# Biases of batch 1's 64-head attention: added by VectorE after the projection, or put into PSUM by one-row matmuls ahead of it

## The chip, the core and the metric

The kernel runs on one core of a Trainium2 chip. The metric is the device time of one execution in microseconds (us). TensorE (PE) does the matmuls and writes to PSUM, VectorE (DVE) and ScalarE (ACT) read PSUM and SBUF, GpSimd (POOL) works on SBUF, SyncE (SP) issues the DMAs. Each engine takes its instructions strictly in the order in which the program gives them to it, and waits on semaphores where the code says `wait_ge`.

## The reference, cut to what matters

Two layers of a perceiver, on x of 2 batches x 256 rows x 256 columns, with a context of 2 x 4096 x 256. Layer 0 is cross attention over the context, then the 64-head linear attention of this case, then a coupled feed-forward; layer 1 is cross attention, a 16-head attention and a mixture of experts. The attention that is changed:

```
def _L0_attn_ref(x, Wq, bq, Wk, bk, Wv, bv, Wo, bo, beta):    # x is layernorm(x)
    q = heads(x @ Wq.T + bq)          # 64 heads of 4
    k = heads(x @ Wk.T + bk)
    v = heads(x @ Wv.T + bv)
    be = jnp.exp(beta)
    q = jax.nn.softmax(be * q, axis=-1)
    k = jax.nn.softmax(be * k, axis=-1)
    kv = jnp.cumsum(jnp.einsum('zsD,zsd->zsDd', k, v), axis=1)
    kn = jnp.cumsum(k, axis=1)
    num = jnp.einsum('zsD,zsDd->zsd', q, kv)
    den = jnp.sum(q * kn, axis=-1, keepdims=True)
    out = num / den
    return out @ Wo.T + bo
```

## The kernel before

The five engines have one program each. The long stages are the two cross attentions, `attend(0)` and `attend(1)`, whose order is a list written out by hand (`ORDER`); smaller jobs are written as generators and are advanced a step at a time at places given by tables. Between `attend(0)` and `attend(1)` stands `between`: it advances two jobs in turn by a string for each engine (`BETWEEN`), "a" for a step of `attention1` (the 64-head attention of batch 1, `linear_attention(1)`), "y" for a step of `side0` (what is left of batch 0: the end of its feed-forward, then its query projection for layer 1). On TensorE, `between` also puts in matmuls on a tile of ones (`keep_busy`, the tile `ones` of type f16), whose results are not used.

`linear_attention(b)` works on two tiles (t = 0, 1) of 128 rows. In order:

- VectorE: layernorm (statistics, then, after GpSimd's `rstd`, the normalized `xn`, line 1401).
- TensorE: `turn_norm` transposes `xn` into a PSUM bank (line 480); VectorE copies it to `xnT` (line 1408).
- TensorE: values of both tiles (line 525, 4 matmuls of 256 columns) into bank b1; queries and keys (line 528, 2 matmuls of 512 columns for each tile) into bank b0 for t = 0 and b2 for t = 1. Semaphore `a_qkv` rises once for each tile. An f32 matmul appears as two passes (rows) in the trace, a transpose as one.
- VectorE, for each tile: values plus bias into `v2` (line 1449), queries and keys plus bias into `qk2[t]` (line 1450), maximum over each head's 4 elements (line 1454), that subtracted (line 1455, raises `a_sub`).
- ScalarE, for each tile: Exp of `qk2[t]` in place (line 1045, raises `a_exp`).
- VectorE, for each tile: keys' sums, reciprocal and scaling (lines 1461 to 1463, raises `a_soft`). The first of the three waits for `a_exp`.
- GpSimd: the products of keys and values, `F2` (line 1307). TensorE: their cumulative sums (line 542). VectorE: lines 1475 to 1483. TensorE: transposes (line 549) and the output projection (line 555).

For batch 1 the banks b0, b1, b2 are 4, 5 and 6. Banks 1 and 6 are also accumulators of `attend(0)`; they come free when `acc_free` reaches NU.

The feed-forward of batch 0 stands between these steps. Its last cycle has four matmul stages (lines 574, 585, 592, 601) with a ScalarE activation behind each (Gelu at lines 1069, 1076 and 1082, Tanh at line 1092), and then VectorE's lines 1515 to 1518. On ScalarE the Tanh of line 1092 stands directly ahead of the Exp of line 1045, with a table load between the two.

Of the kernel before, what the change touches and what calls it, by code (L numbers as in the profile page):

```python
# [19 lines left out]
ALU = mybir.AluOpType  # L20
ACT = mybir.ActivationFunctionType
AX = mybir.AxisListType
# [4 lines left out]
P = 128  # L27
B, SEQ, D = 2, 256, 256
# [8 lines left out]
NU = NT  # L37
# [126 lines left out]
def acc_bank(u):  # L164

    return 6 if u % 2 == 0 else 1

def side_banks(what, b=0):  # L170
    return (4, 5, 6) if (what, b) == ("a", 1) else (4, 5, 7) if what == "x" or (what, b) == ("l", 1) else (2, 3, 7)
# [34 lines left out]
def build(nc, x, ctx, consts, cols, w_x, w_a, w_ao, b_a, w_f1, w_f2, w_f3, w_f4, w_g1, w_g2, w_g3, w_y, w_yv, b_yv,  # L206
          w_l, w_vo, w_in, w_out, rows6, w_gate, w_e1, b_e1, w_e2, b_e2, consts6, out):
    with ExitStack() as stack:
# [256 lines left out]
        def _(pe):  # L465
# [6 lines left out]
            def turn_norm(what, b):  # L472

                k = NORM[what, b]
                pe.wait_ge(s("xn"), k + 1)
                if k == 0:
                    pe.wait_ge(s("const_in"), 32)
                for c in range(DC):
                    for t in range(2):
                        mm = pe.transpose(ps[:, side_banks(what, b)[0], (c * 2 + t) * P:(c * 2 + t + 1) * P],  # L480
                                          xn_of(what, b)[:, t, c * P:(c + 1) * P], ident)
                mm.then_inc(s("xn_turned"), 1)
# [30 lines left out]

            def linear_attention(b):
                b0, b1, b2 = side_banks("a", b)
                yield
                yield
                turn_norm("a", b)
                yield
                pe.wait_ge(s("xnT"), NORM["a", b] + 1)  # L520
                pe.wait_ge(s("wa_in"), 48)
                lhs = lambda t, c: xnT[:, c, t * P:(t + 1) * P]
                for t in range(2):
                    for c in range(DC):
                        pe.matmul(ps[:, b1, t * D:(t + 1) * D], lhs(t, c), wa[:, c, 512:768], start=(c == 0), stop=(c == DC - 1))
                for t in range(2):
                    for c in range(DC):
                        mm = pe.matmul(ps[:, b0 if t == 0 else b2, :], lhs(t, c), wa[:, c, 0:512],
                                       start=(c == 0), stop=(c == DC - 1))
                    mm.then_inc(s("a_qkv"), 1)  # L530
                    yield
                for _ in range(LA_WAIT):
                    yield
                for t in range(2):

                    pe.wait_ge(s("a_F"), 2 * b + t + 1)
                    for i, (o, f) in enumerate(((ps[:, b0, :], lambda r: F2[:, r, 0:512]), (ps[:, b1, :], lambda r: F2[:, r, 512:1024]),
                                                (ps[:, b2, 0:D], lambda r: qk2[r][:, D:2 * D]))):
                        if t:
                            pe.wait_ge(s("a_o"), 8 * b + i + 1)  # L540
                            pe.matmul(o, ones[:, :], f(0), start=True, stop=False)
                        pe.matmul(o, tri, f(t), start=(t == 0), stop=True).then_inc(s("a_cum"), 1)
                    yield
                    yield
                    yield
                pe.wait_ge(s("a_o"), 8 * b + 8)
                for c in range(DC):
                    for t in range(2):
                        mm = pe.transpose(ps[:, b0, (c * 2 + t) * P:(c * 2 + t + 1) * P], v2[:, t, c * P:(c + 1) * P], ident)
                mm.then_inc(s("a_oT_ps"), 1)  # L550
                yield
                pe.wait_ge(s("a_oT"), b + 1)
                for t in range(2):
                    for c in range(DC):
                        mm = pe.matmul(ps[:, b1, t * D:(t + 1) * D], t2[:, (c * 2 + t) * P:(c * 2 + t + 1) * P], wao[:, c, :],
                                       start=(c == 0), stop=(c == DC - 1))
                mm.then_inc(s("a_out"), 1)
                yield
# [464 lines left out]
        def _(act):  # L1023
# [13 lines left out]
            def linear_attention(b):  # L1037
                yield
                yield
                yield  # L1040
                yield
                for t in range(2):
                    yield
                    act.wait_ge(s("a_sub"), 2 * b + t + 1)
                    act.activation(qk2[t], qk2[t], ACT.Exp, scale=becol).then_inc(s("a_exp"), 1)
                for _ in range(LA_WAIT - 1):
                    yield
                for t in range(2):
                    yield
                    yield  # L1050
                    yield
                act.wait_ge(s("a_oT_ps"), b + 1)
                act.activation(t2, ps[:, side_banks("a", b)[0], :], ACT.Copy).then_inc(s("a_oT"), 1)
                yield
                yield
# [307 lines left out]
        def _(dve):  # L1363
# [73 lines left out]
            def linear_attention(b):  # L1437
                b0, b1, b2 = side_banks("a", b)
                dve.wait_ge(s("wa_in"), 48)
                yield from layernorm("a", b)  # L1440
                yield
                turned("a", b)
                yield
                heads4 = lambda t: qk2[t].rearrange("p (g d) -> p g d", d=D2)
                for t in range(2):

                    n = 2 * b + t
                    dve.wait_ge(s("a_qkv"), n + 1)
                    dve.tensor_tensor(v2[:, t, :], ps[:, b1, t * D:(t + 1) * D], ba[:, 512:768], ALU.add)
                    link(dve.tensor_tensor(qk2[t], ps[:, b0 if t == 0 else b2, :], ba[:, 0:512], ALU.add))  # L1450
                    yield
                    if n:
                        dve.wait_ge(s("a_sub"), n)
                    link(dve.tensor_reduce(s2[:, :], heads4(t), AX.X, ALU.max))
                    publish(dve.tensor_tensor(heads4(t), heads4(t), s2[:, :].unsqueeze(2).broadcast_to([P, P, D2]), ALU.subtract), "a_sub")
                yield
                for t in range(2):

                    dve.wait_ge(s("a_exp"), 2 * b + t + 1)
                    keys, ksum = heads4(t)[:, H2:2 * H2, :], s2[:, 0:H2]  # L1460
                    link(dve.tensor_reduce(ksum, keys, AX.X, ALU.add))
                    link(dve.reciprocal(ksum, ksum))
                    publish(dve.tensor_tensor(keys, keys, ksum.unsqueeze(2).broadcast_to([P, H2, D2]), ALU.mult), "a_soft")
                    yield
                for _ in range(LA_WAIT - 3):
                    yield
                for t in range(2):
                    n = 2 * b + t
                    q4 = qk2[t][:, 0:D].rearrange("p (h a) -> p h a", a=D2)
                    t4 = t2.rearrange("p (h d a) -> p h d a", a=D2, d=D2)  # L1470
                    for half in range(2):
                        hs = slice(half * 32, half * 32 + 32)
                        cum = ps[:, (b0, b1)[half], :].rearrange("p (h d a) -> p h d a", a=D2, d=D2)
                        dve.wait_ge(s("a_cum"), 3 * n + half + 1)
                        publish(dve.tensor_tensor(t4, cum, q4[:, hs, :].unsqueeze(2).broadcast_to([P, 32, D2, D2]), ALU.mult), "a_o")
                        link(dve.tensor_reduce(v2[:, t, half * P:(half + 1) * P], t2.rearrange("p (g a) -> p g a", a=D2), AX.X, ALU.add))
                        yield
                    dve.wait_ge(s("a_cum"), 3 * n + 3)
                    publish(dve.tensor_tensor(t2[:, 0:D], ps[:, b2, 0:D], qk2[t][:, 0:D], ALU.mult), "a_o")
                    link(dve.tensor_reduce(s2[:, 0:H2], t2[:, 0:D].rearrange("p (h a) -> p h a", a=D2), AX.X, ALU.add))  # L1480
                    link(dve.reciprocal(s2[:, 0:H2], s2[:, 0:H2]))
                    v3 = v2[:, t, :].rearrange("p (h d) -> p h d", d=D2)
                    publish(dve.tensor_tensor(v3, v3, s2[:, 0:H2].unsqueeze(2).broadcast_to([P, H2, D2]), ALU.mult), "a_o")
                    yield
                yield
                dve.wait_ge(s("a_out"), b + 1)
                xs = X[:, 2 * b:2 * b + 2, :]
                dve.wait_ge(s("x_bo"), b + 1)
                link(dve.tensor_tensor(xs, xs, bank(b1, a=2), ALU.add))
                yield  # L1490
# [479 lines left out]
```

## Time and profile before

| | |
|---|---|
| median of 3 runs | 568.9 us (568.12 to 569.2) |
| the profiled execution's own time | 568.82 us |
| its span, first to last instruction | 566.9 us |
| TensorE busy | 521.0 us (92%) |
| VectorE busy | 356.4 us (63%) |
| ScalarE busy | 280.4 us (49%) |
| GpSimd busy | 75.6 us (13%) |
| mean granted TensorE clock | 0.981 |

The time lies 1.9 us above the span; what comes before the first and after the last instruction is in it. Busy shares are means over the whole span. The work that is changed lies between 164 and 200 us.

### The profile page before, as it was taken

What the parts mean: (1) busy time and instruction counts of PE and PEld (TensorE: products, weight loads), DVE (VectorE), ACT (ScalarE), POOL (GpSimd) and SP (SyncE); (2) the same over time, 40 slices, a digit from 0 to 9 for tenths busy, and PEclk for the clock granted to TensorE, in tenths of its full rate; (3) what the DMA queues carried; (4) which work ended last, traced back from release to release, by engine and by line L of the source; (5) the groups of instructions that cost most, each with busy time, mean ns of one, the idle gap of its engine ahead of it and who ended that gap; (6) DMA issues with size and microseconds to landing.
All of it is one profiled execution on the core that took longest, in us unless ns stands there. A gap on an engine that the chain in (4) does not pass through costs nothing.

```text
span 566.9 us, 9396 instructions
## 1 busy us (share of the span) xinstructions
PE 521.0 (92%) x3556; PEld 358.0 (63%) x3556; DVE 356.4 (63%) x855; ACT 280.4 (49%) x608; POOL 75.6 (13%) x66
## 2 busy tenths in 40 slices
PE   8799998998998999999989989799999999887992
PEld 6455664565666655657545767688888778664551
DVE  4774646963647864475465565788878787744335
ACT  3676862536632037484367736788855444011110
POOL 0025041200011100000002220323201111200001
PEclk9999999997999999999999999999999999979997
DMA  8974552000000010000410040223183005950001
GB/s 270 304 210 89 113 122 64 1 2 1 1 0 1 1 28 0 1 2 0 163 62 1 1 150 1 75 61 90 52 317 139 1 1 195 348 201 1 1 0 39
DMA packets 45198, 44.07 MB, mean 78 GB/s; under 512 B 18656, under 2 KB 41184, under 8 KB 45024
## 3 DMA queue, kind: packets, MB, share of 16 engines
q1 hardware_dynamic: 45152, 43.45, 25.0%
q8 instruction: 29, 0.48, 0.3%
q14 instruction: 17, 0.14, 0.1%
HBM read 38.73 MB, written 0.52 MB: 69 GB/s over the span
## 4 chain that ended last, share of the span: by engine, by line
PE 65%; DVE 17%; issue 10%; ACT 5%; POOL 1%; DMA 1%; SPq 0%; DVEq 0%; ACTq 0%; POOLq 0%
PE ps L648 10%; PE ps L677 8%; PE ps L785 7%; PE ps L801 7%; PE ps L662 4%; PE ps L679 4%; PE ps L770 3%; PE ps L951 3%; PE ps L736 3%; PE ps L976 2%; PE ps L758 2%; PE ps L871 1%; DVE mx L1541 1%; PE ps L497 1%; PE ps L574 1%
## 5 line engine op out<-in xcount | busy, mean ns | idle before, releaser
L648 PE MATMUL ps<-ctx_tr,qtl 128*128 128x512 f16 x384 | 91.2, 379 | 2.4 <-ACT arena L1126 1.9
L1541 DVE TENSOR_REDUCE mx<-arena 128x1 f32<-128x512 f32 x64 | 43.2, 682 | 32.2 <-ACT arena L1126 31.9
L648 PEld LDWEIGHTS ps<-ctx_tr,qtl 128*128 128x128 f16 x384 | 36.6, 98 | 41.1 <-issue 5.1
L677 PE MATMUL ps<-ctx_nat,pth 128*128 128x512 f16 x172 | 59.5, 385 | 0.0
L1126 ACT ACTIVATE arena<-ps 128x512 f32<-128x512 f32 x64 | 38.0, 595 | 41.2 <-PE ps L648 41.0
L1111 ACT ACTIVATE arena<-arena,small 128x512 f32<-128x512 f32 x64 | 45.7, 714 | 6.6 <-DVE small L1550 6.5
L679 PE MATMUL ps<-ctx_nat,ptl 128*128 128x256 f16 x172 | 47.5, 276 | 0.0
L801 PE MATMUL ps<-arena,ctx_tr 128*128 128x256 f16 x384 | 47.2, 273 | 0.1
L1555 DVE TENSOR_TENSOR ptl<-ps,pth 128x512 f16<-128x512 f32 x43 | 29.5, 688 | 26.6 <-ACT pth L1119 26.5
L662 PE MATMUL ps<-const,arena 128*128 128x128 f32 x256 | 39.4, 277 | 4.3 <-ACT arena L1111 3.0
L1290 POOL TENSOR_TENSOR rstd<-mv,col 128x2 f32<-128x2 f32 x13 | 9.0, 694 | 245.1 <-DVE mv L1395 245.0
L801 PEld LDWEIGHTS ps<-arena,ctx_tr 128*128 128x128 f16 x384 | 37.5, 98 | 4.6 <-DVE ctx_tr L1708 0.3
L662 PEld LDWEIGHTS ps<-const,arena 128*128 128x128 f32 x256 | 30.4, 142 | 15.5 <-ACT arena L1111 7.0
L1197 ACT ACTIVATE pth<-ps 128x512 f16<-128x512 f32 x32 | 19.0, 594 | 33.3 <-PE ps L770 33.3
L470 PE MATMUL ps<-ones 128*128 128x256 f16 x244 | 32.2, 293 | 1.1 <-DVE ones L1886 1.1
L1190 ACT ACTIVATE ctx_tr<-ps,small 128x256 f32<-128x256 f32 x64 | 29.6, 470 | 5.7 <-DVE work L1647 5.6
L1119 ACT ACTIVATE pth<-ps 128x512 f16<-128x512 f32 x43 | 25.4, 590 | 14.1 <-PE ps L662 14.0
L470 PEld LDWEIGHTS ps<-ones 128*128 128x128 f16 x244 | 25.5, 106 | 6.6 <-DVE ones L1886 1.1
L677 PE MATMUL ps<-ctx_nat,arena 128*128 128x512 f16 x84 | 29.1, 385 | 0.0
L1647 DVE TENSOR_SCALAR_CACHE_REDUCE work<-ps 128x256 f16<-128x256 f32 x64 | 24.4, 418 | 6.4 <-PE ps L758 6.3
L677 PEld LDWEIGHTS ps<-ctx_nat,pth 128*128 128x128 f16 x172 | 17.0, 99 | 17.2 <-issue 1.9
L1555 DVE TENSOR_TENSOR arena<-ps,arena 128x512 f16<-128x512 f32 x21 | 14.5, 689 | 20.4 <-ACT arena L1119 20.3
(293 smaller groups left out, 1039.4 us busy)
## 6 DMA issues: line engine op xcount, KB each, us to landing
ctx_nat<-in_w_e SPq DMA_DIRECT2D x8, 1024.0 KB, 7.5
ctx_tr<-in_w_e SPq DMA_DIRECT2D x6, 1024.0 KB, 11.5
work<-in_ctx SPq DMA_DIRECT2D x8, 512.0 KB, 5.4
ctx_tr<-in_ctx SPq DMA_DIRECT2D x8, 512.0 KB, 7.3
work<-in_w_vo SPq DMA_DIRECT2D x8, 512.0 KB, 3.9
ctx_nat<-in_w_l SPq DMA_DIRECT2D x4, 512.0 KB, 5.2
arena<-in_w_e SPq DMA_DIRECT2D x2, 1024.0 KB, 7.4
wts<-in_rows SPq DMA_DIRECT2D x1, 1024.0 KB, 14.5
```

What stands on the lines that cost most here:

```text
L470: pe.matmul(ps[:, to, 0:SEQ], o[:, 0:P], o, start=True, stop=True, skip_group_check=True)
L648: mm = pe.matmul(ps[:, n % 2, :], qtl[:, qh, d, u * P:(u + 1) * P], CT[:, t0:t0 + KT, kh, d, :], start=(i == 0 and d == 0), stop=(i == 2 a ...
L662: mm = pe.transpose(ps[:, 4 + j % 2, i * P:(i + 1) * P], S[:, (j) % SRING, i * P:(i + 1) * P], ident)
L677: pe.matmul(ps[:, acc, :], PH[j % PRING][:, i * P:(i + 1) * P], CN[:, t].rearrange("p h d -> p (h d)"), start=(c == 0 and i == 0), stop=Fa ...
L679: mm = pe.matmul(ps[:, acc, 0:D], PL[j % PRING][:, i * P:(i + 1) * P], CN[:, t, 0, :], start=False, stop=(c == NCH - 1 and i == KT - 1), s ...
L785: mm = pe.matmul(ps[:, 4 + i % 2, d * SEQ:(d + 1) * SEQ], xl5[b][:, xh, u, d * P:(d + 1) * P], pt[:, i % 2, pu], start=(n == 0), stop=(n = ...
L801: mm = pe.matmul(ps[:, 6 + b, t * D:(t + 1) * D], oT5[:, i % 2, oh, c, p * P:(p + 1) * P], vo[:, h, vh, c, :], start=(i % H5 == 0 and p == ...
L1111: act.activation(S[:, j % SRING, :], S[:, j % SRING, :], ACT.Exp, bias=ebias[:, u:u + 1], scale=SCALES[L], accum_out=ls[:, u, c:c + 1]).th ...
L1126: act.activation(S[:, n % SRING, :], ps[:, n % 2, :], ACT.Copy).then_inc(s("score_copied"), 1)
L1190: act.activation(P5[:, i % 2, t, :], ps[:, i % 2, t * SEQ:(t + 1) * SEQ], ACT.Exp, bias=nb5[:, i % 2, t:t + 1], scale=1.0 / 16, accum_out= ...
L1541: dve.tensor_reduce(mx[:, u, c:c + 1], S[:, n % SRING, :], AX.X, ALU.max).then_inc(s("score_max"), 1)
L1555: dve.tensor_tensor(PL[j % PRING], ps[:, 4 + j % 2, :], PH[j % PRING], ALU.subtract).then_inc(s("pt_lo"), 1)
```

## The change

For batch 1 alone, the biases bq, bk and bv (row 0 of `ba`, columns 0 to 768) are written into the PSUM banks by four matmuls of one row (`ones[0:1, :]` by a piece of the bias row), and the projections accumulate on top of them. Queries and keys of t = 0 go to bank 1 in place of bank 4. VectorE takes the maximum, and subtracts it, straight from PSUM. The values are copied from PSUM to `v2` by ScalarE. TensorE gets a wait for `acc_free` (banks 1 and 6 must be free) ahead of the four matmuls, and a wait for both Exps ahead of the cumulative sum that overwrites bank b1.

```diff
+QK_BANK = 1
...
             def linear_attention(b):
                 b0, b1, b2 = side_banks("a", b)
-                yield
-                yield
+                first = QK_BANK if b else b0
+                yield
+                yield
+                if b:
+                    pe.wait_ge(s("acc_free"), NU)
+                    row = lambda a, z: ba[0:1, a:z]
+                    for to, a, z in ((ps[:, b1, 0:D], 512, 768), (ps[:, first, :], 0, 512), (ps[:, b2, :], 0, 512)):
+                        pe.matmul(to, ones[0:1, :], row(a, z), start=True, stop=False, skip_group_check=True)
+                    pe.matmul(ps[:, b1, D:2 * D], ones[0:1, :], row(512, 768), start=False, stop=False, skip_group_check=True)
                 turn_norm("a", b)
                 yield
                 pe.wait_ge(s("xnT"), NORM["a", b] + 1)
...
-                        pe.matmul(ps[:, b1, t * D:(t + 1) * D], lhs(t, c), wa[:, c, 512:768], start=(c == 0), stop=(c == DC - 1))
+                        pe.matmul(ps[:, b1, t * D:(t + 1) * D], lhs(t, c), wa[:, c, 512:768], start=(c == 0 and b == 0), stop=(c == DC - 1),
+                                  skip_group_check=True)
...
-                        mm = pe.matmul(ps[:, b0 if t == 0 else b2, :], lhs(t, c), wa[:, c, 0:512],
-                                       start=(c == 0), stop=(c == DC - 1))
+                        mm = pe.matmul(ps[:, first if t == 0 else b2, :], lhs(t, c), wa[:, c, 0:512],
+                                       start=(c == 0 and b == 0), stop=(c == DC - 1), skip_group_check=True)
...
+                        if b and not t and i == 1:
+                            pe.wait_ge(s("a_exp"), 2 * b + 2)
...
                 for t in range(2):
+                    if b:
+                        act.wait_ge(s("a_qkv"), 2 * b + t + 1)
+                        act.activation(v2[:, t, :], ps[:, side_banks("a", b)[1], t * D:(t + 1) * D], ACT.Copy)
                     yield
                     act.wait_ge(s("a_sub"), 2 * b + t + 1)
                     act.activation(qk2[t], qk2[t], ACT.Exp, scale=becol).then_inc(s("a_exp"), 1)
...
                     dve.wait_ge(s("a_qkv"), n + 1)
-                    dve.tensor_tensor(v2[:, t, :], ps[:, b1, t * D:(t + 1) * D], ba[:, 512:768], ALU.add)
-                    link(dve.tensor_tensor(qk2[t], ps[:, b0 if t == 0 else b2, :], ba[:, 0:512], ALU.add))
+                    raw = heads4(t)
+                    if b:
+                        raw = ps[:, QK_BANK if t == 0 else b2, :].rearrange("p (g d) -> p g d", d=D2)
+                    else:
+                        dve.tensor_tensor(v2[:, t, :], ps[:, b1, t * D:(t + 1) * D], ba[:, 512:768], ALU.add)
+                        link(dve.tensor_tensor(qk2[t], ps[:, b0 if t == 0 else b2, :], ba[:, 0:512], ALU.add))
...
-                    link(dve.tensor_reduce(s2[:, :], heads4(t), AX.X, ALU.max))
-                    publish(dve.tensor_tensor(heads4(t), heads4(t), s2[:, :].unsqueeze(2).broadcast_to([P, P, D2]), ALU.subtract), "a_sub")
+                    link(dve.tensor_reduce(s2[:, :], raw, AX.X, ALU.max))
+                    publish(dve.tensor_tensor(heads4(t), raw, s2[:, :].unsqueeze(2).broadcast_to([P, P, D2]), ALU.subtract), "a_sub")
```

The order of TensorE's instructions in the stage between the two cross attentions, before. L470 are the matmuls on the tile of ones, L574 to L601 belong to the feed-forward of batch 0, L480 are the transposes of `xn` of batch 1, L525 and L528 its projection (one row here is one matmul of the program, an f32 one being two passes in the trace):

```order
L574 MATMUL ps<-arena,wts 128x256 x4
L470 MATMUL ps<-ones 128x256 x6
L585 MATMUL ps<-wts 128x256 x2
L480 MATMUL ps<-const,work 128x128 x4
L592 MATMUL ps<-wts 64x256
L525 MATMUL ps<-arena,work 128x256 x4
L528 MATMUL ps<-arena,work 128x512 x4
L601 MATMUL ps<-wts 128x256
```

The same place on TensorE in the changed kernel, whose line numbers are higher (L598 was L585, L483 was L480, L614 was L601):

```order
L587 MATMUL ps<-arena,wts 128x256 x4
L473 MATMUL ps<-ones 128x256 x6
L598 MATMUL ps<-wts 128x256 x2
L526 MATMUL ps<-wts,ones 128x256
L526 MATMUL ps<-wts,ones 128x512 x2
L527 MATMUL ps<-wts,ones 128x256
L483 MATMUL ps<-const,work 128x128 x4
L605 MATMUL ps<-wts 64x256
L535 MATMUL ps<-arena,work 128x256 x4
L539 MATMUL ps<-arena,work 128x512 x4
L614 MATMUL ps<-wts 128x256
```

The four bias matmuls (L526, L527) stand between the second feed-forward stage and the transposes; nothing else moved on TensorE.

The order of ScalarE's instructions at the same place, before (L1069 to L1092 are the feed-forward's activations, L1045 the Exps, L1053 the copy behind the transposes of line 549):

```order
L1069 ACTIVATE wts<-ps,col 128x256 x2
L1076 ACTIVATE wts<-ps,col 128x256
L1082 ACTIVATE wts<-ps,col 64x256
L1092 ACTIVATE wts<-ps,small 128x256
L1045 ACT_TABLE_LOAD
L1045 ACTIVATE work<-work,small 128x512 x2
L1053 ACTIVATE work<-ps 128x512
```

And in the changed kernel (L1108 was L1092, L1061 was L1045):

```order
L1085 ACTIVATE wts<-ps,col 128x256 x2
L1092 ACTIVATE wts<-ps,col 128x256
L1098 ACTIVATE wts<-ps,col 64x256
L1108 ACTIVATE wts<-ps,small 128x256
L1058 ACTIVATE work<-ps 128x256
L1061 ACT_TABLE_LOAD
L1061 ACTIVATE work<-work,small 128x512
L1058 ACTIVATE work<-ps 128x256
L1061 ACTIVATE work<-work,small 128x512
L1069 ACTIVATE work<-ps 128x512
```

The copy of the first tile's values (L1058) stands between the Tanh and the table load, that of the second tile between the two Exps.

## Rows read from the trace of the kernel before

**Rows 1.** The page: engines' busy time, and the chain that ended last by engine.

```profile
PE 521.0 (92%) x3556; PEld 358.0 (63%) x3556; DVE 356.4 (63%) x855; ACT 280.4 (49%) x608; POOL 75.6 (13%) x66
PE 65%; DVE 17%; issue 10%; ACT 5%; POOL 1%; DMA 1%; SPq 0%; DVEq 0%; ACTq 0%; POOLq 0%
```

**Rows 2.** The chain in order of time, 164 to 180 us: start, duration, what.

```profile
168.14 0.74 DVE work L1401 x2
168.93 0.67 PE ps L480 x4
...
170.37 1.99 PE ps L525 x8
172.37 1.73 PE ps L528 x4
...
179.12 0.43 DVE s L1461
```

**Rows 3.** Timeline of TensorE, 166 to 196 us: start, duration, line, operation.

```profile
167.84 1.03 PE L585 MATMUL ps<-wts 128*128 128x256 f32 x4
...
172.20 3.60 PE L528 MATMUL ps<-arena,work 128*128 128x512 f32 x8
175.73 0.70 PE L601 MATMUL ps<-wts 64*128 64x256 f32 x2
176.36 6.50 PE L470 MATMUL ps<-ones 128*128 128x256 f16 x58
```

**Rows 4.** Timeline of ScalarE, 166 to 196 us.

```profile
176.46 0.47 ACT L1092 ACTIVATE wts<-ps,small 128x256 f32<-128x256 f32 x1 [5.79 <-PE ps L601]
176.96 1.28 ACT L1045 ACT_TABLE_LOAD   x1
178.25 0.72 ACT L1045 ACTIVATE work<-work,small 128x512 f32<-128x512 f32 x1
179.12 0.72 ACT L1045 ACTIVATE work<-work,small 128x512 f32<-128x512 f32 x1
```

**Rows 5.** Timeline of VectorE, 166 to 196 us.

```profile
174.12 0.42 DVE L1449 TENSOR_TENSOR work<-ps,wts 128x256 f32<-128x256 f32 x1 [3.80 <-PE ps L528]
174.46 0.68 DVE L1450 TENSOR_TENSOR work<-ps,wts 128x512 f32<-128x512 f32 x1
175.18 0.69 DVE L1454 TENSOR_REDUCE s<-work 128x128 f32<-128x512 f32 x1
175.90 0.69 DVE L1455 TENSOR_TENSOR work<-work,s 128x512 f32<-128x512 f32 x1
176.62 0.42 DVE L1449 TENSOR_TENSOR work<-ps,wts 128x256 f32<-128x256 f32 x1
```

**Rows 6.** The chain, 150 to 205 and 199 to 230 us.

```profile
184.50 0.43 DVE s L1461
...
200.69 0.67 PE ps L549 x4
...
204.03 7.77 PE ps L648 x36
```

**Rows 7.** Groups by line and shape, 160 to 205 us: busy us, mean ns of one.

```profile
L528 PE MATMUL ps<-arena,work 128*128 128x512 f32 x8 | 3.6, 592 | 0.0
...
L601 PE MATMUL ps<-wts 64*128 64x256 f32 x4 | 1.4, 428 | 0.0
...
L585 PE MATMUL ps<-wts 128*128 128x256 f32 x4 | 1.0, 380 | 0.0
```

**Rows 8.** Timeline of ScalarE, 214 to 226 us: two activations back to back, and one alone.

```profile
216.66 0.84 ACT L1069 ACTIVATE work<-ps,col 128x256 f32<-128x256 f32 x2
...
218.35 0.47 ACT L1076 ACTIVATE work<-ps,col 128x256 f32<-128x256 f32 x1 [0.22 <-PE ps L585]
```

**Rows 9.** Stretches: PE, PEld, DVE, ACT, POOL busy, granted clock, DMA share, GB/s.

```profile
180.00:184.00 4.00, 2.86 (x27) 2.31 (x24) 3.86 (x6) 0.00 (x0) 2.01 (x1) 1.00 0.00 0
...
500.00:505.00 5.00, 5.00 (x21) 3.62 (x20) 2.15 (x7) 0.00 (x0) 0.21 (x1) 0.54 0.90 347
```

## The prediction, made before the changed kernel ran

> **What bounds the kernel now.** I read the page first. TensorE is busy 92% of the span, and the chain of work that ended last is TensorE for 65% and VectorE for 17% of it [rows 1]. That is a mean over stages, so it doesn't say what the edited stage waits for. I went on to the chain in order of time around the edit. At 168 us it goes from the layernorm (L1401) to TensorE's transposes (L480), which start at 168.93, then through the projection (L525, L528). From there on it is VectorE's, until L1461 at 179.12 and beyond [rows 2]. VectorE's own timeline shows why: it waits 3.80 us for L528, starts L1449 at 174.12 and from there its instructions stand end to end [rows 5]. The chain leaves VectorE for TensorE's L549 only at 200.69, and the scores of the next cross attention (L648) start at 204.03 [rows 6], behind all of this in TensorE's program. So a microsecond that L1461 starts later is a microsecond later for the rest of the kernel.
>
> The third view is ScalarE's timeline. Its Exp of the first tile ends at 178.25 + 0.72 = 178.97, only 0.15 before VectorE starts L1461, which needs it. And this Exp does not start when its data is there: it stands behind the Tanh (176.46), which waited 5.79 us for TensorE's L601, and behind a table load of 1.28 [rows 4]. L601 in turn is behind the projection, at 175.73 [rows 3]. So two paths end at L1461 nearly together: projection, VectorE's eight instructions, L1461; and projection, L601, Tanh, table load, Exp, L1461. A gain on the first one alone is worth at most 0.15 us.
>
> **The change part by part.**
>
> *Taken from VectorE.* L1449 and L1450 of both tiles. From L1449's start to L1454's start are 175.18 - 174.12 = 1.06 us [rows 5], twice 2.12 us. This is on the first path only.
>
> *VectorE reads PSUM for the maximum and the subtraction.* No reduction from PSUM is in these rows. The nearest: L1450 reads 512 f32 columns from PSUM in 0.68, L1455 the same amount from SBUF in 0.69, L1454 reduces from SBUF in 0.69 [rows 5]. I take no difference; the upper bound, a doubled reduction, would add 0.7 for each tile and, as is shown below, would still be covered.
>
> *Four bias matmuls on TensorE.* They are eight passes: four of 256 columns and four of 512. Four passes of 256 columns (L585) took 1.03 with one alone at 0.380, so the step from one to the next is (1.03 - 0.38) / 3 = 0.217. Eight passes of 512 took 3.60 with one at 0.592: (3.60 - 0.59) / 7 = 0.430 [rows 3, 7]. Sum: 4 x 0.217 + 4 x 0.430 = 2.59 us. Those are passes over 128 rows, and these have one. The nearest row with fewer is L601: 64 rows, 256 columns, 428 ns mean for one, against 380 with 128 rows [rows 7]. Half the rows made it no shorter, so I take the full price. The bounds are zero, if a pass costs by rows, and, if the eight do not overlap at all, 4 x 0.380 + 4 x 0.592 = 3.89 us.
>
> The Trainium skill bears on this step ("TensorE: Matmul & The Clock Gate", § Why this matters for your kernels): its row on small contractions says that one matmul of 32 rows takes as long as one of 128. The trace shows the same for 64 rows, and nothing in it reaches down to one row. By the page the bias passes cost the full 2.59 and the kernel is slower; by a price that goes by rows they would be nearly free.
>
> *Where do they lie?* In TensorE's order they are behind L585 and ahead of L480. L585's last pass starts at about 167.84 + 3 x 0.217 = 168.49, so the first bias pass can start at 168.71. `acc_free` is no wait, since VectorE publishes it before it begins this layernorm. The passes end their turn at 168.71 + 2.59 = 171.30, and L480, which was ready at 168.93 [rows 2, 3], starts then: 2.37 us late. Only 0.22 us is hidden, in the gap between the two. TensorE has no idle time here that could take the rest; the layernorm it used to wait for is what the passes now overlap, and it is nearly over. Everything behind L480 moves by 2.37: the copy to `xnT`, L525, L528, and L601 too.
>
> *The copy of the values on ScalarE.* The first one stands behind the Tanh and ahead of the table load, thus on the second path. Two such activations back to back took 0.84, one alone 0.47: one more costs 0.37 [rows 8]. (0 if it were covered, 0.5 if it did not overlap the Tanh.) The second copy stands between the two Exps: the second Exp ended at 179.84 [rows 4], and its reader is VectorE's second L1461 at 184.50 [rows 6]. It has 4.7 us, and needs no more than a few tenths of them. The new wait of TensorE for both Exps is far behind them and costs nothing.
>
> *The sum at L1461.* Second path: the Exp ends at 178.97 + 2.37 + 0.37 = 181.71, and VectorE starts some 0.03 later, at 181.74. First path: the second tile's projection ended at 172.20 + 3.60 = 175.80, now 178.17, and then come one reduction and one subtraction, 2 x 0.72: 179.61. VectorE therefore waits 2.1 us for the Exp: what it saves turns into this wait, and a slower read of PSUM would vanish in it. L1461 starts at 181.74 in place of 179.12: **+2.62 us**. Terms: 2.37 (bias passes) + 0.37 (copy) + 0.03 (hand-over) - 0.15 (VectorE had been the later one). From there VectorE's instructions are the same, and so are TensorE's behind them.
>
> The profiled execution took 568.82 us, 0.08 under the median of 568.9. 568.82 + 2.62 = 571.44, from the median 571.52. I say **571.5 us**, 0.46% slower.
>
> **The rivals.** What a measurement of this kernel can tell from no change I take as 0.2%, 1.14 us.
>
> *Passes of one row are cheap* (10%). For it: they multiply 1/128 of the cells, and no row is under 64 rows. Against it: L601. With a price of zero the Exp still gets the copy: 0.37 + 0.03 - 0.15 = +0.25, 569.1 us, no change. It becomes a measurable loss once the eight passes cost over 1.1 us.
>
> *The delay is taken up later* (3%). A wait for something that did not move, say a DMA, would absorb it. The chain has 1% of DMA in all [rows 1], and the transfers behind 204 us are issued on semaphores of the work itself. Result within 1.1 us of 568.9.
>
> *The bias passes don't overlap one another* (6%). Weights of one row might not be loaded ahead. 3.89 in place of 2.59 gives +3.92: 572.7 us.
>
> *TensorE's clock falls in this stretch* (3%). It was granted in full here, with TensorE busy 2.86 of 4 us at the loosest place; at 500 to 505 us it was 0.54, near 1.2 GHz [rows 9]. If the bias passes, L525 and the first half of L528 ran at half speed, they would take 2.59 + 1.99 + 1.73 = 6.3 us more: about 577.7 us.
>
> *The saving on VectorE comes through: faster* (4%). The mechanism: the Exp isn't the gate, because ScalarE has its table loaded and the Tanh done early. The place is L1461; the price is the first path alone. With bias passes at their full price that path gives 179.61, +0.49; it ends on the fast side only if they cost less than 1.9 us as well. At zero it gives 175.82 + 1.44 = 177.26, 1.86 earlier: 567.0 us. The point from which it decides: the Exp would have to end by 177.3, 1.7 us before its row, but the Tanh alone ended at 176.93 and the load takes 1.28 [rows 4]. That is why it gets little; part of the 4% is for something in a later stage that falls better by luck.
>
> **How the numbers follow.** The forecast holds 74%; its own range is 570.8 to 572.3, from the copy's bounds (0 to 0.5), the spread of the three runs of before, and some tenths for the stages behind. Adding the case without overlap makes 80%; the edges of the cheap-pass case are reached from 570.2. So the range is 570.2 to 573.0. Slower by over 0.2%: 74 + 6 + 3 = 83%. Within 0.2%: 10 + 3 = 13%. Faster: 4%.
>
> **What the profile after would show.** The eight bias passes between L585's and L480's counterparts, 0.22 and 0.43 apart, and the transposes starting near 171.3 (right), or within 0.3 of 169 (the cheap-pass case). VectorE's first reduction starting near 176.5 and its duration near 0.69. The Tanh near 178.8, the copy, the table load near 179.7, the Exp to 181.7. An idle time of VectorE of about 2.1 us that ends with the Exp, ahead of L1461's counterpart: this is the step that says the saving is lost. If VectorE has no such wait, the reading of the two paths is wrong. The scores of the next cross attention start near 206.6. The prediction fails if a one-row pass costs much less than a full one, or if the clock moves.

## The result, and the profile after

The changed kernel took 574.91 us (median of 11 runs, 570.65 to 576.66), the kernel before 568.66 us (median of 11 runs): ratio 1.0101, 95% interval 1.0083 to 1.0119, 1.0% slower. Predicted were 571.5 us, in a range of 570.2 to 573.0. The direction was right and the size was not: the loss is 6.25 us where 2.6 were forecast, 2.4 times as much. Two executions far outside the rest, of two kernels of the experiments, are left out of what follows: one of 909 us at a clock of 0.55 throughout, and one of 2511 us.

The 11 runs fall into two groups. Four of them (570.65, 571.02, 571.44, 572.52 us) have a mean granted TensorE clock of 0.981 to 0.982; seven (574.4 to 576.66 us) have 0.972 to 0.976. The profiled execution (574.40 us) is one of the seven. The middle of the four, 571.23, is 2.6 us above the kernel before, which is what was forecast. Whether those four escaped the cost that is found below is not shown, since none of them was profiled.

The page of the changed kernel: busy time by engine, the granted clock in 40 slices, the chain that ended last by engine.

```profile
PE 526.6 (92%) x3564; PEld 361.1 (63%) x3564; DVE 354.7 (62%) x851; ACT 280.8 (49%) x610; POOL 75.7 (13%) x66
...
PEclk9999999998998999999999989999999999989997
...
PE 74%; DVE 15%; ACT 6%; issue 3%; POOL 1%; DMA 1%; SPq 0%; DVEq 0%; ACTq 0%; POOLq 0%
```

Against [rows 1] TensorE is busy 5.6 us longer and VectorE 1.7 us less. A slice is 14.3 us wide, and the 8 in the thirteenth (172 to 186 us) is at the changed place, where the kernel before had full clock.

TensorE's timeline of the changed kernel, 164 to 206 us: start, duration, line.

```profile
165.78 1.03 PE L598 MATMUL ps<-wts 128*128 128x256 f32 x4
166.74 2.41 PE L526 MATMUL ps<-wts,ones 1*128 1x256 f32 x6
169.00 0.76 PE L527 MATMUL ps<-wts,ones 1*128 1x256 f32 x2
169.69 1.11 PE L483 MATMUL ps<-const,work 128*128 128x128 f32 x4
...
171.78 3.78 PE L535 MATMUL ps<-arena,work 128*128 128x256 f32 x8
175.36 3.98 PE L539 MATMUL ps<-arena,work 128*128 128x512 f32 x8
179.26 0.70 PE L614 MATMUL ps<-wts 64*128 64x256 f32 x2
```

The eight bias passes (L526 and L527, one row, `1*128`) stand between the feed-forward's stage and the transposes, and the first six of them run at the pace that was worked out: L526's start to L527's is 2.26 us. Then everything gets slow. The transposes (L483) take 1.11 in place of 0.67, and the eight passes over the values (L535) 3.78 in place of 1.99 [rows 2]. L539 takes 3.98 in place of 3.60 [rows 3], and what follows it is at the old pace again.

The same stretches by window, with the granted clock third from the end.

```profile
168.00:170.00 2.00, 2.00 (x7) 0.87 (x6) 0.00 (x0) 0.00 (x0) 0.17 (x1) 0.82 0.00 0
170.00:172.00 2.00, 2.00 (x7) 0.91 (x6) 0.69 (x1) 0.11 (x1) 0.00 (x0) 0.50 0.00 0
172.00:174.00 2.00, 2.00 (x5) 1.63 (x6) 0.00 (x0) 0.36 (x1) 0.00 (x0) 0.50 0.04 8
174.00:176.00 2.00, 2.00 (x5) 1.35 (x4) 0.00 (x0) 0.00 (x0) 0.00 (x0) 0.50 0.00 0
176.00:180.00 4.00, 4.00 (x11) 1.55 (x10) 1.96 (x3) 0.00 (x1) 0.00 (x0) 0.99 0.00 0
```

The clock is 0.50, the lower level of 1.2 GHz, from about 169.3 to 176 us. It fell while the bias passes ran, and TensorE was busy the whole time: 2.00 of 2 us in each window, and 4.00 of 4 from 160 to 164 and from 164 to 168 us too. So it isn't idleness that took the clock. At another place a fall does come behind idle time: in the kernel before TensorE is busy 2.44 us of the 4 from 132 to 136 us, and the clock is 0.50 from 136 to 140.

VectorE's and then ScalarE's timeline of the changed kernel. L1424 is the copy behind the transposes (before: L1408), L1474 the reduction from PSUM (L1454), L1481 the keys' sums (L1461); L1108 is the Tanh (L1092), L1058 the new copy, L1061 the Exp (L1045).

```profile
170.84 0.69 DVE L1424 COPY work<-ps 128x512 f32<-128x512 f32 x1 [4.01 <-PE ps L483]
177.65 0.69 DVE L1474 TENSOR_REDUCE s<-ps 128x128 f32<-128x512 f32 x1 [6.12 <-PE ps L539]
...
179.43 0.69 DVE L1474 TENSOR_REDUCE s<-ps 128x128 f32<-128x512 f32 x1 [0.35 <-PE ps L539]
...
182.87 0.42 DVE L1481 TENSOR_REDUCE s<-work 128x64 f32<-128x256 f32 x1 [2.03 <-ACT work L1061]
```

```profile
180.00 0.48 ACT L1108 ACTIVATE wts<-ps,small 128x256 f32<-128x256 f32 x1 [7.64 <-PE ps L614]
180.37 0.38 ACT L1058 ACTIVATE work<-ps 128x256 f32<-128x256 f32 x1
180.75 1.28 ACT L1061 ACT_TABLE_LOAD   x1
182.05 0.72 ACT L1061 ACTIVATE work<-work,small 128x512 f32<-128x512 f32 x1
```

The four adds are gone and the reduction from PSUM takes 0.69, as from SBUF [rows 5]. And VectorE then stands still for 2.03 us until the Exp ends: that is what the removed adds became. Of VectorE's waits, the two for the transposes and for the projection have grown, to 4.01 and 6.12 us (from 0.75 and 3.80), and the 2.03 is new.

GpSimd's timeline is a good ledger of the whole program, since it has few instructions and they are the same ones in both kernels. Before, then after (L1290 and L1306 are the layernorms' `rstd`, L1307 and L1323 the product of keys and values):

```profile
167.42 0.69 POOL L1290 TENSOR_TENSOR rstd<-mv,col 128x2 f32<-128x2 f32 x1 [39.70 <-DVE mv L1395]
...
180.67 2.01 POOL L1307 TENSOR_TENSOR work<-work 128x1024 f32<-128x1024 f32 x1 [10.44 <-DVE work L1463]
...
335.22 0.69 POOL L1290 TENSOR_TENSOR rstd<-mv,col 128x2 f32<-128x2 f32 x1 [5.92 <-DVE mv L1395]
351.94 1.16 POOL L1337 TENSOR_TENSOR arena<-work,arena 128x512 f16<-128x512 f32 x1 [16.03 <-ACT arena L1171]
```

```profile
165.37 0.69 POOL L1306 TENSOR_TENSOR rstd<-mv,col 128x2 f32<-128x2 f32 x1 [38.11 <-DVE mv L1411]
...
184.41 2.01 POOL L1323 TENSOR_TENSOR work<-work 128x1024 f32<-128x1024 f32 x1 [16.24 <-DVE work L1483]
...
338.99 0.69 POOL L1306 TENSOR_TENSOR rstd<-mv,col 128x2 f32<-128x2 f32 x1 [5.93 <-DVE mv L1411]
357.28 1.16 POOL L1353 TENSOR_TENSOR arena<-work,arena 128x512 f16<-128x512 f32 x1 [17.60 <-ACT arena L1187]
```

From the `rstd` of batch 1's attention to its first product, which I call **the stretch** from here on, it was 180.67 - 167.42 = 13.25 us and is 184.41 - 165.37 = 19.04: +5.79. From there to 335.22 or 338.99 both take the same to 0.03. The rest of the ledger lies in code that is the same in both: the stretch began 2.05 us earlier in this execution, and from 339 to 357 us 1.57 are lost, while the clock is 0.57 at 336 to 340 us. Such stretches of low clock are in the kernel before too, at 136 to 144 and 496 to 508 us, and their place and length differ from one profile to the next. What one is worth can be read from the same ledger: between GpSimd's `rstd` at 127 us and the one that opens the stretch, the kernel before took 40.41 us with the low clock at 136 to 144; four kernels of the experiments, whose code there is the same and whose profiles have full clock there, took 37.36 to 37.38. That is 3.0 us for one fall.

Two cautions follow. The kernel before itself ran in 565.12 to 570.85 us on one chip. With 5.79 us added that is 570.9 to 576.6, nearly all that the changed kernel's 11 runs cover, so its two groups can come from the falls elsewhere as well as from the stretch. And the loss at 336 us is in the four profiles with eight f32 bias passes (0.57 to 0.62 in a window of 4 us) and in none of the other seven; with one profile of each kernel no run says whether that is chance.

### The profile page after: what moved, and what is told of

It is laid out like the page before. It is cut to its first block, busy times and chain, and to the rows that moved or that the text cites. A ratio compares the mean times of both kernels' runs of the same rounds, so it can differ in the third digit from the quotient of the medians.

```text
span 572.6 us, 9409 instructions
## 1 busy us (share of the span) xinstructions
PE 526.6 (92%) x3564; PEld 361.1 (63%) x3564; DVE 354.7 (62%) x851; ACT 280.8 (49%) x610; POOL 75.7 (13%) x66
## 4 chain that ended last, share of the span: by engine, by line
PE 74%; DVE 15%; ACT 6%; issue 3%; POOL 1%; DMA 1%; SPq 0%; DVEq 0%; ACTq 0%; POOLq 0%
PE ps L661 10%; PE ps L690 10%; PE ps L798 7%; PE ps L814 7%; PE ps L675 5%; PE ps L692 5%; PE ps L749 3%; PE ps L783 3%; PE ps L964 3%; PE ps L989 2%; PE ps L587 2%; PE ps L771 2%; PE ps L884 1%; DVE mx L1561 1%; PE ps L598 1%
## 5 line engine op out<-in xcount | busy, mean ns | idle before, releaser
L1306 POOL TENSOR_TENSOR rstd<-mv,col 128x2 f32<-128x2 f32 x13 | 9.0, 696 | 243.1 <-DVE mv L1411 243.0
```

## The experiments

Theory 1: passes that feed one row into the array do not keep TensorE's clock up, and this is the part of the loss that the forecast lacked. Theory 2: the rest is as forecast, that is, the passes' turn on TensorE costs 2.4 us, and VectorE's saving is lost because the Exp gates it. In the medians below "before" is the kernel before on the same chip. The stretch is read from the one profile of each kernel, and so is the clock in it.

**Bias passes alone, on the kernel before.** VectorE's adds stay; the one-row matmuls write banks that nobody reads.

```diff
+                if b:
+                    pe.wait_ge(s("acc_free"), NU)
+                    for to, a, z in ((ps[:, 1, 0:D], 512, 768), (ps[:, 1, :], 0, 512), (ps[:, 6, :], 0, 512), (ps[:, 1, 0:D], 512, 768)):
+                        pe.matmul(to, ones[0:1, :], row(a, z), start=True, stop=True, skip_group_check=True)
                 turn_norm("a", b)
```

> The kernel before, with all its VectorE adds, and with the wait and four one-row matmuls of the same sizes ahead of the transposes; they write PSUM banks that are overwritten or unused, so nothing of the result changes. Theory 1: the passes alone bring both costs, 2.4 us of TensorE's turn and, in most runs, the clock: runs at about 571.1 us (568.7 + 2.37) and runs at about 574.7. Rival (the accumulation on top of the bias, or the PSUM reads, matter): 571.1 us or less in all runs, with the clock at 1.00 from 168 to 180 us.

Measured: 574.07 us (6 runs) against 568.61, ratio 1.0082 (1.0050 to 1.0113). Four runs at 573.97 to 575.41 and two at 570.26 and 571.35: two groups again. The stretch took 18.83 us, +5.58. Its clock, by window:

```profile
168.00:172.00 4.00, 4.00 (x12) 1.74 (x10) 0.52 (x1) 0.00 (x0) 0.69 (x1) 0.71 0.00 0
172.00:176.00 4.00, 4.00 (x11) 2.87 (x10) 0.17 (x1) 0.47 (x1) 0.00 (x0) 0.50 0.01 4
```

The passes alone bring both costs, the turn and the clock. Accumulating on top of them and reading PSUM are not needed for either.

**The same passes over 128 rows.** The identity by the bias rows, which stand in all 128 partitions of `ba`, gives the same sum.

```diff
-                    row = lambda a, z: ba[0:1, a:z]
+                    row = lambda a, z: ba[:, a:z]
...
-                        pe.matmul(to, ones[0:1, :], row(a, z), start=True, stop=False, skip_group_check=True)
+                        pe.matmul(to, ident, row(a, z), start=True, stop=False, skip_group_check=True)
```

> The changed kernel, with the same eight bias passes at the same place, but over 128 rows: the identity by the bias rows that stand in all 128 partitions of the bias tile. The result is the same. Theory 1 (TensorE's clock fell because of passes that feed one row): the granted clock stays 1.00 from 168 to 180 us, the first reduction from PSUM starts 2.4 us later after the layernorm than in the kernel before, and every run is 2 to 3.2 us above the kernel before, about 571.3 us, with none near 575. Rival (the clock fell for another cause, such as a stretch without matmuls nearby or the new wait): 575 us in more than half of the runs and a clock near 0.5 behind the bias passes, as in the changed kernel (574.9 us median).

Measured: ratio 1.0047 (1.0023 to 1.0071) against 568.61 us, seven runs between 569.22 and 572.92 us and none near 575. Its profiled execution was the one of 909 us, so the kernel was run again.

> The same kernel as the one with bias passes over 128 rows, for a profile at full clock. Theory 1 (the clock fell because the passes feed one row): clock 1.00 from 168 to 180 us, the transposes 2.4 us later after the layernorm, the Exp ends 2.7 us later, runs around 571.5 us. Rival: a clock near 0.5 right behind the bias passes and runs near 575.

Measured: 571.48 us (6 runs) against 568.19, ratio 1.0071 (1.0044 to 1.0099), the slowest at 573.96. TensorE's timeline and one window of it:

```profile
165.33 2.31 PE L526 MATMUL ps<-wts,const 128*128 128x256 f32 x6
167.48 0.59 PE L527 MATMUL ps<-wts,const 128*128 128x256 f32 x2
167.91 0.60 PE L483 MATMUL ps<-const,work 128*128 128x128 f32 x4
...
169.30 1.99 PE L535 MATMUL ps<-arena,work 128*128 128x256 f32 x8 [0.21 <-DVE work L1424]
```

```profile
168.00:172.00 4.00, 3.79 (x18) 2.48 (x17) 0.69 (x1) 0.47 (x1) 0.00 (x0) 1.00 0.02 4
```

The clock is 1.00 and L535 takes 1.99 again. The stretch took 15.75 us, +2.50, against a forecast of +2.62. The program is the same but for what the bias passes read, the identity and 128 bias rows in place of a row of ones and one bias row: 19.04 - 15.75 = 3.29 us is what the fall of the clock cost in the profiled execution. TensorE is busy no more here (3.79 of 4 us), and this kernel has one non-zero weight in a column, just as the one-row passes have. What differs is the rows that are fed. The times bear it out: the interval of the changed kernel, 1.0083 to 1.0119, does not meet that of the first of these two experiments, 1.0023 to 1.0071, and meets that of the second, 1.0044 to 1.0099, only at its upper end.

**64 rows.** The upper half of the identity by 64 bias rows; rows 64 to 127 of each tile get no bias.

```diff
+                        pe.matmul(to, const[0:64, 0, :], ba[0:64, a:z], start=True, stop=False, skip_group_check=True)
```

> The changed kernel with the eight bias passes over 64 rows: half of the identity by 64 bias rows, so that rows 64 to 127 of each tile of batch 1 get no bias. The passes take as long as with one row or 128. Theory 1: the clock stays up, as with 128 rows, about 571.3 us; should it fall as with one row, some runs near 575 us, so the number of rows between one and 64 isn't what tells, and only full passes keep it. Rival of e1: 575 us here as there.

Measured: 571.97 us (6 runs, 571.02 to 573.6) against 568.61, ratio 1.0063 (1.0043 to 1.0084); clock 1.00 in the stretch, which took 16.10 us, +2.85. The passes and what follows them cost 0.35 more here than with 128 rows. Where between one row and 64 it turns was not tried.

**No bias matmuls at all.** The changed kernel without them and their wait: bq, bk and bv of batch 1 are left out.

```diff
-                if b:
-                    pe.wait_ge(s("acc_free"), NU)
...
-                    pe.matmul(ps[:, b1, D:2 * D], ones[0:1, :], row(512, 768), start=False, stop=False, skip_group_check=True)
```

> The changed kernel without the bias matmuls and their wait: the biases bq, bk, bv of batch 1 are left out. VectorE's four adds are gone, ScalarE's copy stands ahead of the table load. Theory 1 (Tanh, copy, table load, Exp gate VectorE, its saving becomes a wait): 568.7 + 0.25 = 568.9 us, within 0.6; VectorE idles about 1.6 us ahead of its keys' sums, ended by the Exp. Rival (the saving counts): 566.8 us, and no such wait.

Measured: 568.24 us (12 runs) against 568.61, ratio 1.0006 (0.9987 to 1.0024). Four adds fewer on VectorE, and nothing gained. The stretch took 13.47 us, +0.22, and VectorE's timeline has the wait:

```profile
179.40 0.42 DVE L1475 TENSOR_REDUCE s<-work 128x64 f32<-128x256 f32 x1 [2.02 <-ACT work L1055]
```

I had written 1.6 us for this wait; it is 2.02. Its end is what counts, and the stretch moved by 0.22 where 0.25 was expected.

**The feed-forward's last matmul ahead of the projection, on the kernel before.** This takes the Exp out of VectorE's way.

```diff
                         pe.matmul(ps[:, b1, t * D:(t + 1) * D], lhs(t, c), wa[:, c, 512:768], start=(c == 0), stop=(c == DC - 1))
+                if b:
+                    yield
                 for t in range(2):
...
-    "aayyayaaaayyyyayaaayyaaay",
+    "aayyayayaaaayyyayaaayyaaay",
```

> The kernel before, with one move: the feed-forward's last matmul (line 601) stands ahead of the projection of queries and keys, not behind it. Its Tanh and the table load then run while the projection does, so the Exp no longer waits for them. Theory 2 (two paths of nearly equal length, the adds on VectorE being the other): the projection comes 0.43 us later, VectorE is never stopped by the Exp, and the time is 568.6 + 0.43 = 569.0 us. Rival (the Exp was what held VectorE in the kernel before): faster than before by over 1 us.

Measured: 569.66 us (12 runs, 566.2 to 573.88) against 568.19, ratio 1.0029 (1.0005 to 1.0053), where 569.0 us was expected: not faster, so the Exp was not what held the kernel before. But the move costs more than 0.43. The stretch took 14.08, +0.83, and VectorE's wait for the projection grew from 3.80 [rows 5] by 0.82:

```profile
171.87 0.42 DVE L1451 TENSOR_TENSOR work<-ps,wts 128x256 f32<-128x256 f32 x1 [4.62 <-PE ps L530]
```

So this matmul of 64 rows among ones of 128 cost its two passes, 0.43 us, and some 0.4 us at the seams.

**The change with cheap passes.** Biases as f16 high and low halves, made by GpSimd and stacked on partitions 0 to 63 and 64 to 127, against a tile of 1/64: four f16 passes over all 128 rows. They replace the six matmuls on the tile of ones ahead of line 585's stage. First with line 601's matmul where it was.

```diff
+                    pe.wait_ge(s("b16"), 3)
+                    for to, a, z in ((ps[:, b1, 0:D], 512, 768), (ps[:, first, :], 0, 512), (ps[:, b2, :], 0, 512)):
+                        pe.matmul(to, inv64[:, :], ba16[:, a:z], start=True, stop=False, skip_group_check=True)
...
+            pool.memset(inv64[:, :], 1.0 / 64).then_inc(s("b16"), 1)
+            pool.tensor_copy(ba16[:, :], ba[:, 0:3 * D]).then_inc(s("b16"), 1)
+            pool.wait_ge(s("b16"), 2)
+            pool.tensor_tensor(ba16[64:128, :], ba[64:128, 0:3 * D], ba16[64:128, :], ALU.subtract).then_inc(s("b16"), 1)
```

> As the f16 version, but with line 601's matmul where it was, behind the projection. Theory 2: the Exp gates VectorE again, with the values' copy ahead of the table load: 568.6 + 0.25 = 568.9 us, and VectorE waits some 1.6 us for the Exp. Rival (the place of the matmul doesn't matter): the same time as the version with it moved, 567.2 us.

Measured: 569.15 us (12 runs) against 568.19, ratio 1.0035 (1.0011 to 1.0059); 568.9 was expected. The stretch took 13.47, +0.22, just as without biases: the passes are free, VectorE's saving is still lost, and it waits 2.03 us for the Exp.

**The same with line 601's matmul early.**

> The changed kernel, with the biases as f16 high and low halves (made by GpSimd long before, high on partitions 0 to 63, low on 64 to 127, against a tile of 1/64), so four f16 passes over 128 rows in place of eight; they stand in the place of six matmuls on the tile of ones, ahead of line 585's stage; and line 601's matmul ahead of the projection of queries and keys. Theory 2: the passes cost nothing (0.64 us in place of 0.64), the gate is lifted, VectorE's saving counts: 0.43 later for the projection, then 179.12 - 177.7 = 1.4 us earlier at the keys' sums, 567.2 us. Rival (the saving is lost for another reason): 568.6 or more.

Measured: 570.57 us (12 runs) against 568.19, ratio 1.0047 (1.0024 to 1.0070). A miss in the whole, where 567.2 was expected, though the stretch took 12.30, 0.95 less than before: the gate is lifted and the saving counts, less the 0.8 of the moved matmul. A loss lies 40 us earlier, in both f16 kernels: from the `rstd` at 127 us to the stretch this one took 42.55 us, 2.14 more than the kernel before with the same fall of the clock on the way. This is VectorE's normalization for the feed-forward in the one of the experiment ahead, beside GpSimd's new work (it took 0.73 before):

```profile
127.72 2.75 DVE L1425 TENSOR_SCALAR wts<-X,mv,rstd 128x256 f32<-128x256 f32 x2 [0.24 <-POOL rstd L1308]
```

GpSimd's cast and subtraction, 0.82 and 1.64 us, held VectorE for 2.0 us. The kernel before has the same at another place: its L1515 took 0.41 us at 162.58 and 2.20 at 180.62, beside GpSimd's product of 2.01. The Trainium skill has this ("SBUF — State Buffer", § SBUF: two separate sides): some of VectorE's instructions and GpSimd's lock a shared pair of ports, and whichever comes second blocks until the other's instruction is done; the 2.75 and the 2.20 agree.

**GpSimd's work later.** One wait more, `pool.wait_ge(s("f_gs"), 1)`.

> The f16 version with line 601's matmul early, but GpSimd makes the halves later, after the feed-forward's first Gelu of the context, when VectorE does not run its normalization. In the earlier version that normalization took 2.75 us in place of 0.73 beside GpSimd, and this is where its 2 us went. Theory 2: 0.95 us earlier at the keys' sums, as measured there, and nothing lost elsewhere: about 567.5 us in the median of runs of the kernel before at 568.4. Rival (the loss was in the changed order, or in the clock alone): 569.5 or more, and a normalization that takes 0.73 us with the time no better.

Measured: 568.75 us (12 runs) against 568.25, ratio 1.0008 (0.9989 to 1.0028). The normalization takes 0.74 and the stretch 12.30 again. Against the version ahead 1.9 us came back (0.50 us above the kernel before in place of 2.38), but the 0.95 that the stretch shows is not seen in the median, and the 567.5 expected was missed. Eight of the 12 runs have a clock of 0.981 or less, against 9 of the 23 of the kernel before.

**The values last.** VectorE no longer reads them, so the projection can do queries and keys first. Both copies of the values move between the two Exps, and 16 matmuls on the tile of ones behind the projection are taken out.

```diff
+                if not b:
+                    values_of()
                 for t in range(2):
                     for c in range(DC):
                         mm = pe.matmul(ps[:, first if t == 0 else b2, :], lhs(t, c), wa[:, c, 0:512],
...
+                if b:
+                    values_of()
+                    yield
...
+                    if b and not t:
+                        act.wait_ge(s("b16"), 5)
+                        for r in range(2):
+                            act.activation(v2[:, r, :], ps[:, side_banks("a", b)[1], r * D:(r + 1) * D], ACT.Copy).then_inc(s("b16"), 1)
```

> As that, and the projection of the values is moved behind that of queries and keys, since VectorE no longer reads it; ScalarE copies both tiles' values between its two Exps; 16 fewer matmuls on the tile of ones behind the projection. VectorE starts 1.8 us sooner; the second tile's projection ends at 170.37 + 3.60 + 0.82 = 174.8 in the kernel before's times, the keys' sums start at 176.3 in place of 179.1: 2.8 us earlier, about 565.7 us. Rival (another gate comes up, the copies or GpSimd's product): under 1.5 us of gain.

Measured: 567.05 us (11 runs, without the one of 2511 us) against 568.25, ratio 0.9965 (0.9938 to 0.9992): faster than both kernels, but by 1.2 us and not by the 2.8 expected (565.7 us). GpSimd's timeline of it:

```profile
168.53 0.69 POOL L1317 TENSOR_TENSOR rstd<-mv,col 128x2 f32<-128x2 f32 x1 [29.45 <-DVE mv L1431]
...
179.10 2.01 POOL L1336 TENSOR_TENSOR work<-work 128x1024 f32<-128x1024 f32 x1 [7.76 <-DVE work L1503]
```

The stretch is 10.57 us, 2.68 less than before, against 2.8 expected at the keys' sums; why the time shows less than half of it was not settled. The idea of the change pays with three things done to it: passes that are short and full of rows, the Tanh out of the way, and the projection in the order in which its readers need it. The last was tried only on top of the other two.

## Why the prediction was right in part, and wrong

| | stretch, us | against before | clock in it | time, ratio |
|---|---|---|---|---|
| before | 13.25 | | 1.00 | |
| changed kernel | 19.04 | +5.79 | falls to 0.50 | 1.0101 |
| one-row passes alone | 18.83 | +5.58 | falls to 0.50 | 1.0082 |
| 64 rows | 16.10 | +2.85 | 1.00 | 1.0063 |
| 128 rows | 15.75 | +2.50 | 1.00 | 1.0047, 1.0071 |
| no bias | 13.47 | +0.22 | 1.00 | 1.0006 |
| line 601's matmul early, alone | 14.08 | +0.83 | 1.00 | 1.0029 |
| f16 passes | 13.47 | +0.22 | 1.00 | 1.0035 |
| f16 passes, matmul early | 12.30 | -0.95 | 1.00 | 1.0047 |
| the same, GpSimd's work later | 12.30 | -0.95 | 1.00 | 1.0008 |
| values last | 10.57 | -2.68 | 1.00 | 0.9965 |

- *What bounds the kernel: two paths that meet at L1461.* Right. Without the Exp's gate, no gain (early matmul); without VectorE's adds, no gain either (no bias); with both lifted, 0.95 us less in the stretch.
- *Price of a one-row pass: in full.* Right: 2.26 us from the first pass to the seventh, six passes, where the forecast's steps give 2 x 0.217 + 4 x 0.430 = 2.15. The row on small contractions that the prediction cited from the Trainium skill ("TensorE: Matmul & The Clock Gate", § Why this matters for your kernels) holds for this time down to one row.
- *Where they lie: transposes 2.37 late.* Right where the clock stays up. With 128 rows the transposes start 167.91 - 164.78 = 3.13 us after the normalization, where it was 0.79 [rows 2]: 2.34 late.
- *VectorE's reads of PSUM: no difference.* Right, 0.69.
- *The wait in place of the adds, 2.1.* Right, 2.03.
- *The copy, 0.37, and the hand-over, 0.03.* Both off, and they cancel by luck. The copy's row is 0.38 long, but what it adds is the time from the Tanh's start to the table load's: 180.75 - 180.00 = 0.75 us, where it was 176.96 - 176.46 = 0.50 [rows 4]. So it cost 0.25. The Exp ends at 182.05 + 0.72 = 182.77 and VectorE starts at 182.87: the hand-over is 0.10.
- *The sum, +2.62.* Right with 128 rows (+2.50); wrong for the changed kernel, whose profile has another term. Its stretch is longer by 5.79 us, and its median by 6.25.
- *TensorE's clock falls in this stretch (3%).* This is the step that failed: the sum has nothing for it. The prediction gave it 3% because the clock was granted in full here "with TensorE busy 2.86 of 4 us at the loosest place": it took TensorE's busy time for what holds the clock. The bias passes keep TensorE busy in full, 4.00 of 4 us, and the clock falls to 0.50 all the same; this costs 3.29 us. The price that the rival named was too high as well, 6.3, mostly since it had the bias passes themselves (2.59 of it) run at half speed. They were nearly over when the clock fell. At this point the Trainium skill ("TensorE: Matmul & The Clock Gate", § What's actually happening) says that the gate goes by how busy the engine has been. The trace agrees only if a one-row pass is not counted as busy; by the profile's busy share the rule would have kept the clock.

One slip in the prediction has no weight: in the case of a faster kernel the passes would have to cost less than 2.1 us, not 1.9. The 1.9 is the delay, and 0.22 us of the passes is hidden.

What stays open: how many of the 11 runs lose the clock in the stretch, since one was profiled, and what in the pass the chip counts, rows or something that goes with them. Why the version with GpSimd's work later shows 0.5 us more than the kernel before in the median (interval -0.6 to +1.6) and 0.95 less in the stretch was not settled either. The low clock elsewhere is likely a part of it; at 352 to 360 us its profile has 0.77 and 0.80, where the kernel before has full clock.

## What to carry to other kernels

A matmul with few rows cost as much of TensorE's time as a full one here, and eight passes of one row cost the clock of the work behind them; where a bias is to be put into PSUM, feed all 128 partitions (a bias that is already broadcast, against the identity or a constant tile) and try f16. Before work is taken off an engine, look for the second path into the next instruction that needs it: here it ended 0.15 us before the first one, and the whole saving became a wait. An edit's worth is best read between two instructions that are the same in both kernels, since one fall of the clock elsewhere was worth 3.0 us here, more than the 2.6 that were forecast for the edit.

## What the runs showed of the hardware that was not expected

- Eight one-row f32 passes, 3 us long with TensorE busy throughout, and the granted clock falls to 0.50 for about 7 us, in the profiles of both kernels that have them. With 64 and with 128 rows the clock is 1.00 there, and the slowest of those 19 runs took 573.96 us; of the 17 with one row, 10 took over 574 us.
- A matmul of 64 rows put between matmuls of 128 made its successor's reader wait 0.82 us longer, of which its two passes explain 0.43.
- Low clock in code that the edit does not touch differs between profiles, and one such fall cost 3.0 us. The kernel before ran in 565.12 to 570.85 us on one chip, at mean clocks of 0.988 to 0.978.
